# A macaron block on one core: the guard of the front chunks on ScalarE and GpSimd, four score banks in the last two units, and low parts by a minus-identity matmul

## The reference

```python
x = x + 0.5 * ffn(layernorm(x))     # base 512x512 + bias, and 8 LoRA experts of rank 16, top 2 by a softmax router
x = x + attn(layernorm(x))          # 32 query heads, 8 key/value heads of size 16, softmax over 1024 keys
x = x + 0.5 * ffn(layernorm(x))     # the same weights again

def bitnet_linear(x, weight, scale_param):          # q, k, v and o of the attention
    s = jnp.maximum(jnp.mean(jnp.abs(weight), axis=1), 1e-08)
    y = jnp.einsum('bsi,oi->bso', x, jnp.sign(weight / s[:, None])) * (s * scale_param)[None, None, :]
    return jnp.nan_to_num(y, nan=0.0, posinf=1000000.0, neginf=-1000000.0)
```

## Time and profile before

| what | value |
|---|---|
| median of 3 runs | 1210.61 us (1208.24 to 1212.01) |
| the profiled execution's own time | 1210.39 us |
| its span, first to last instruction | 1208.6 us |
| alone stage, to the first exponential of body 0 | 0 to 238.4 us |
| bodies 0 and 1 | about 119 us each |
| bodies 2 to 6 | about 112 us each |
| units 30 and 31 | 1088.9 to 1140.9 us |
| tail | 1140.9 to 1208.6 us |

### The profile page before, as it was taken

One profiled execution on the slowest core, in us unless ns is written; L12 is line 12 of the kernel. 1 busy time (PEld: TensorE's weight loads), 2 busy tenths in 40 slices (PEclk: granted clock), 3 DMA queues, 4 the chain that ended last, 5 costly groups with the idle time before them and its releaser, 6 DMA issues.

```text
span 1208.6 us, 19276 instructions
## 1 busy us (share of the span) xinstructions
PE 1081.1 (89%) x5944; PEld 491.6 (41%) x5944; DVE 876.0 (72%) x1259; ACT 708.4 (59%) x1313; POOL 306.2 (25%) x527
## 2 busy tenths in 40 slices
PE   1877676699999999999999999999999999999857
PEld 1666564334433342334333433443343334333336
DVE  3676869677787778787778777868886787782164
ACT  2343432365776667676667666756765676668511
POOL 4134345610241033141032104210510241032010
PEclk9997989699999999999999999999999999999968
DMA  7012133121121111300300021103101200200300
...
DMA packets 87331, 59.03 MB, mean 49 GB/s; under 512 B 44144, under 2 KB 73328, under 8 KB 87280
## 3 DMA queue, kind: packets, MB, share of 16 engines
...
...
## 4 chain that ended last, share of the span: by engine, by line
PE 73%; DVE 16%; ACT 5%; issue 3%; POOL 1%; DMA 1%; SPq 0%; DVEq 0%; ACTq 0%; POOLq 0%
PE ps_out L1226 19%; PE ps_score L1214 18%; PE ps_max L1193 15%; PE ps_fill L1151 6%; DVE neg_max L1015 3%; PE ps_fill L1178 2%; DVE neg_max L1073 2%; ACT probs L786 2%; PE ps_fill L1124 2%; PE ps_out L1151 2%; PE ps_fill L1155 1%; DVE xt_l L968 1%; DVE zd L927 1%; PE ps_fill L1136 1%; PE ps_max L1207 1%
## 5 line engine op out<-in xcount | busy, mean ns | idle before, releaser
L786 ACT ACTIVATE probs<-ps_score 128x512 f32<-128x512 f32 x1024 | 555.8, 595 | 275.1 <-PE ps_score L1214 273.5
L1015 DVE TENSOR_REDUCE neg_max<-ps_max 128x1 f32<-128x1024 f32 x480 | 571.4, 1218 | 175.7 <-PE ps_max L1193 174.6
L1214 PE MATMUL ps_score<-qst,kst 99*128 99x512 bf16 x1024 | 319.8, 386 | 11.0 <-ACT probs L786 7.8
L1193 PE MATMUL ps_max<-kst,qst 96*128 96x512 bf16 x1024 | 290.0, 384 | 20.7 <-DVE neg_max L1073 12.4
L1226 PE MATMUL ps_out<-probs,v_ring 128*32 128x512 f32 x2048 | 274.5, 608 | 0.0
L1214 PEld LDWEIGHTS ps_score<-qst,kst 99*128 99x128 bf16 x1024 | 88.1, 97 | 287.6 <-ACT probs L786 243.5
L1193 PEld LDWEIGHTS ps_max<-kst,qst 96*128 96x128 bf16 x1024 | 89.2, 98 | 137.5 <-DVE neg_max L1073 21.8
L307 POOL TENSOR_TENSOR wait_pad<-wait_pad 1x1 bf16<-1x1 bf16 x75 | 16.3, 217 | 395.9 <-DVE neg_max L1015 335.0
L1226 PEld LDWEIGHTS ps_out<-probs,v_ring 128*32 128x32 f32 x2048 | 40.4, 108 | 90.7 <-issue 90.3
L1124 PE MATMUL ps_fill<-ident,xn 128*128 128x128 f32 x192 | 32.1, 292 | 37.1 <-ACT xn L735 25.7
L735 ACT ACTIVATE xn<-xc,ln_shift,rstd 128x512 f32<-128x512 f32 x48 | 38.1, 810 | 41.0 <-POOL ln_shift L574 40.5
...
## 6 DMA issues: line engine op xcount, KB each, us to landing
...
```

What stands on the lines that cost most here:

```text
L786: act.activation(probs[:, kt % 2, j, :], ps_score[j % 2][:, :], ACT.Exp, scale=1.0 / HD ** 0.5).then_inc(probs_ready, 1)
L1015: dve.tensor_reduce(neg_max[:, uu % 2, t:t + 1], ps_max[max_slot(uu, pos)][:, :, :], AXY, ALU.max, negate=True).then_inc(max_read, 1)
L1193: last = pe.matmul(ps_max[slot][:, half, :], qst[0:SR, r, j, q * P:(q + 1) * P], kst[0:SR, r, half * 512:half * 512 + 512], start=True, st ...
L1214: pe.matmul(ps_score[j % 2][:, :], kst[0:SR + PARTS, uu, kt * P:(kt + 1) * P], qst[0:SR + PARTS, uu, j, :], start=True, stop=True).then_in ...
```

## The change

- **Guard of front chunks.** ACT evicts to `zd` instead of `z`, and at C0, C1, C2 writes `z` = minus `zd` (one more ACT instruction of 512 columns). POOL makes `zneg` = clamp of `zd` to `[-BIG, 0]`, `zpos` (the same place as `z`) = clamp of minus `zd` to `[-BIG, 0]`, their difference, and the mask as `zd` times 0. Both clamps are now of the form min, then max. DVE keeps only the predicated copy. This holds for all front chunks: `FRONT_ON_DVE` is empty. S1 and S3 on POOL are three instructions of 512, 512 and 256 columns.
- **Low parts outside the bodies** (alone stage and tail): PE adds minus identity times `xt_h` to the bank, and ACT copies the result to `xt_l`. DVE has no part in it.
- **Units 30 and 31**: scores 2 and 3 of a slot go to the free half of `ps_max`; a score waits for the exponential four before it.
- **Opening**: ACT casts the FFN weights after T1b of chunk 0.0, DVE makes their low parts before the statistics of chunk 0.1. POOL writes `neg_ident`.

```diff
-FRONT_ON_DVE = ("clamp", "sum")
+FRONT_ON_DVE = ()
+        def four_score_banks(i, uu):
+            return isinstance(i, int) and UB * i + uu >= NU - 2
+        def score_bank(i, uu, j):
+            if four_score_banks(i, uu) and j >= 2:
+                return ps_max[1 - turn_slot(uu, True)][:, j - 2, :]
+            return ps_score[j % 2][:, :]
...
+            gp.tensor_scalar(neg_ident[:, :], ident[:, :], -1.0, None, ALU.mult).then_inc(const_ready, 1)
...
+                if ch.front:
+                    gp.wait_ge(negated[s], ch.n * 3 + piece + 1)
+                    gp.tensor_scalar(zneg[s][:, cols], zd[s][:, cols], 0.0, -BIG, ALU.min, ALU.max).then_inc(clamped[s], 1)
+                    gp.tensor_scalar(zpos[s][:, cols], z[s][:, cols], 0.0, -BIG, ALU.min, ALU.max).then_inc(clamped[s], 1)
+                    return
...
+                if ch.front:
+                    gp.tensor_tensor(zpos[s][:, cols], zneg[s][:, cols], zpos[s][:, cols], ALU.subtract).then_inc(clamp_sum[s], 1)
+                    return
...
+                    not_finite(ch, k)
...
+                    for a0 in range(0, KQ, 512):
+                        piece = slice(a0, min(a0 + 512, KQ))
+                        rest = kq[:, piece] if k == 1 else parts[s][:, 2, piece]
+                        last = gp.tensor_tensor(rest, kq[:, piece], parts[s][:, k - 1, piece], ALU.subtract)
...
+                if ch.alone and pos[2:] in ("al", "bl"):
+                    stage, t = pos[:3], "ab".index(pos[2])
+                    act.wait_ge(low_ready[s], ch.low0 + ch.tn(stage) + 1)
+                    act.activation(xt_l[s][:, :, t * P:(t + 1) * P],
+                                   ps_fill[ch.bank(stage)[0]][:, :].rearrange("p (c n) -> p c n", c=DC),
+                                   ACT.Copy).then_inc(filler_read[ch.bank(stage)[0]], 1)
...
+                if pos in ("C0", "C1", "C2") and ch.front:
+                    k = int(pos[1])
+                    cols = slice(512 * k, 512 * k + 512)
+                    bnk, reads = ch.bank(("VK", "Q0", "Q1")[k])
+                    act.wait_ge(filler_read[bnk], reads + 1)
+                    act.activation(z[s][:, cols], zd[s][:, cols], ACT.Copy, scale=-1.0).then_inc(negated[s], 1)
...
-                if step[0] == "G" and ch.front:
-                    dve.wait_ge(clamp_sum[s], ch.sum0 + (k + 1))
-                    dve.tensor_scalar(mask, z[s][:, cols].bitcast(I32), INF_BITS, INF_BITS, ALU.bitwise_and,
-                                      ALU.bitwise_xor).then_inc(guard_step[s], 1)
...
-                        dve.copy_predicated(zd[s][:, cols], mask, z[s][:, cols]).then_inc(guard_step[s], 1)
+                        dve.copy_predicated(zd[s][:, cols], mask, zpos[s][:, cols]).then_inc(guard_step[s], 1)
...
+                if ch.alone and pos[2:] in ("al", "bl"):
+                    stage, t = pos[:3], "ab".index(pos[2])
+                    pe.wait_ge(xt_h_ready[s], ch.t0 + ch.tn(stage) + 1)
+                    pe.matmul(ps_fill[ch.bank(stage)[0]][:, :].rearrange("p (c n) -> p c n", c=DC), neg_ident[:, :],
+                              xt_h[s][:, :, t * P:(t + 1) * P], start=False, stop=True,
+                              skip_group_check=True).then_inc(low_ready[s], 1)
+                    return
...
+                if four_score_banks(i, uu) and kt == 0 and j >= 2:
+                    pe.wait_ge(max_read, max_use(i, 1, 16) + 1 if uu == 2 else turn_use(i, 2, True) + 1)
+                elif four_score_banks(i, uu) and kt > 0:
+                    pe.wait_ge(probs_ready, i * (32 * UB) + (32 * uu + 4 * kt + j - 3))
```

More of the change, by code:

```diff
@@ L37 @@
 BIG = 1e6
-INF_BITS = 0x7F800000
 KQ = CH + DC * CH
@@ L154, in macaron @@
         identb = sb("identb", [P, P], BF16)
+        neg_ident = sb("neg_ident", [P, P], F32R)
         ones = sb("ones", [P, P], F32)
@@ L217, in macaron @@
         z = [t[:, 0:ZW] for t in zm]
+        zpos = z
         zneg = [t[:, ZW:2 * ZW] for t in zm]
@@ L271, in macaron @@
         bias_added = [sem(f"bias_added{s}") for s in range(2)]
+        low_ready = [sem(f"low_ready{s}") for s in range(2)]
         xt_h_ready = [sem(f"xt_h_ready{s}") for s in range(2)]
@@ L280, in macaron @@
         guard_step = [sem(f"guard_step{s}") for s in range(2)]
+        negated = [sem(f"negated{s}") for s in range(2)]
+        mask_ready = [sem(f"mask_ready{s}") for s in range(2)]
         part_cast = [sem(f"part_cast{s}") for s in range(2)]
@@ L620, in not_finite @@
                 gp_wait(gp, clamp_sum[s], ch.sum0 + (piece + 1))
-                gp.tensor_scalar(zneg[s][:, cols], z[s][:, cols], 0.0, 0.0, ALU.mult, ALU.add).then_inc(guard_step[s], 1)
+                value = zd[s] if ch.front else z[s]
+                gp.tensor_scalar(zneg[s][:, cols], value[:, cols], 0.0, 0.0, ALU.mult, ALU.add).then_inc(mask_ready[s], 1)
             def fill(item):
@@ L635, in fill @@
                     clamped_sum(ch, k)
-                    if not ch.front:
-                        not_finite(ch, k)
-                if pos in ("G0", "G1", "G2") and ch.on_dve("clamp") and not ch.on_dve("sum"):
-                    clamped_sum(ch, int(pos[1]))
+                    not_finite(ch, k)
                 if pos in ("S1", "S3") and not ch.on_dve("split"):
@@ L711, in _, with ffn_weights @@
         def _(act):
-            act.wait_ge(ffn_in, 5 * 16)
-            act.activation(wr_hl[:, :, 0:E], wr_raw[:, :, :], ACT.Copy).then_inc(ffn_hi, 1)
-            for dst, src in ((a_h, raw_a), (wb_h, raw_wb), (b_h, raw_b)):
-                act.activation(dst[:], src, ACT.Copy).then_inc(ffn_hi, 1)
+            def ffn_weights():
+                act.wait_ge(ffn_in, 5 * 16)
+                act.activation(wr_hl[:, :, 0:E], wr_raw[:, :, :], ACT.Copy).then_inc(ffn_hi, 1)
+                for dst, src in ((a_h, raw_a), (wb_h, raw_wb), (b_h, raw_b)):
+                    act.activation(dst[:], src, ACT.Copy).then_inc(ffn_hi, 1)
             def attn_weights():
@@ L758, in fill @@
                         act.wait_ge(parts_stored[s], n * (16 * 2 * PARTS))
-                    act.activation(z[s][:, 0:CH], ps[:, 0:CH], ACT.Copy, scale=col_scale[:, 0:1])
-                    act.activation(z[s][:, CH:2 * CH], ps[:, CH:2 * CH], ACT.Copy,
+                    act.activation(zd[s][:, 0:CH], ps[:, 0:CH], ACT.Copy, scale=col_scale[:, 0:1])
+                    act.activation(zd[s][:, CH:2 * CH], ps[:, CH:2 * CH], ACT.Copy,
                                    scale=col_scale[:, 1:2]).then_inc(filler_read[bnk], 1)
@@ L766, in fill @@
                         a0 = 512 + (m0 + m) * CH
-                        last = act.activation(z[s][:, a0:a0 + CH], ps[:, m * CH:(m + 1) * CH], ACT.Copy,
+                        last = act.activation(zd[s][:, a0:a0 + CH], ps[:, m * CH:(m + 1) * CH], ACT.Copy,
                                               scale=col_scale[:, 2 + m0 + m:3 + m0 + m])
                     last.then_inc(filler_read[bnk], 1)
+                if pos in ("C0", "C1", "C2") and ch.front:
[4 more added lines that the diff above has]
+                    act.activation(z[s][:, cols], zd[s][:, cols], ACT.Copy, scale=-1.0).then_inc(negated[s], 1)
                 if pos == "VT":
@@ L775, in fill @@
                 if pos == "S0":
-                    act.wait_ge(guard_step[s], ch.guard0 + 6)
+                    act.wait_ge(guard_step[s], ch.sum0 + 3)
                     act.activation(parts[s][:, 0, :], zd[s][:, CH:CH + KQ], ACT.Copy).then_inc(part_cast[s], 1)
@@ L785, in exp_tile @@
                     act.wait_ge(probs_used, i * (8 * UB) + (8 * uu + kt - 1))
-                act.activation(probs[:, kt % 2, j, :], ps_score[j % 2][:, :], ACT.Exp,
+                act.activation(probs[:, kt % 2, j, :], score_bank(i, uu, j), ACT.Exp,
                                scale=1.0 / HD ** 0.5).then_inc(probs_ready, 1)
@@ L809, in _ @@
                 fill(item)
+                if item[0].n == 0 and item[1] == "T1b" and item[0].slot == 0:
+                    ffn_weights()
                 if item[0].n == 0 and item[1] == "FFa0" and item[0].slot == 0:
@@ L962, in fill @@
                                           ALU.add).then_inc(bias_added[s], 1)
-                if pos in ("T0al", "T0bl", "T1al", "T1bl", "T2al", "T2bl"):
+                if pos in ("T0al", "T0bl", "T1al", "T1bl", "T2al", "T2bl") and not ch.alone:
                     stage = pos[:3]
@@ L1075, in _ @@
                 fill(item)
-                if item[0].n == 0 and item[0].slot == 1 and item[1] == "LN1c":
+                if item[0].n == 0 and item[0].slot == 0 and item[1] == "T1bl":
                     ffn_weights()
@@ L1091, in _ @@
         def _(pe):
-            pe.wait_ge(const_ready, 12)
+            pe.wait_ge(const_ready, 13)
             def sum_o():
@@ L1123, in fill @@
                     for c in range(DC):
-                        last = pe.transpose(ps[:, c * P:(c + 1) * P], xn[s][:, t, c * P:(c + 1) * P], ident[:, :])
```

(5 more changed lines are left out.)

22 lines of the change are left out of this document (10 added, 12 removed).

## The result

| | before | changed |
|---|---|---|
| median | 1211.31 us (1208.24 to 1212.99, 4 runs) | 1228.01 us (1227.08 to 1231.27, 4 runs) |
| ratio | | 1.0147, 95% interval 1.0129 to 1.0165 |
| the profiled execution, its span | 1210.39, 1208.6 | 1231.27, 1229.4 |

The kernel became 16.7 us slower, where I had forecast 8: the direction was right, the size was not, and 1228 lies outside my range.

What follows compares the result with a forecast made beforehand. DVE was taken to bound the guard stretches and the row maxima. The terms -4.0 + 1.4 + 13.4 - 2.2 - 0.5 - 4.3 + 4.5 gave +8.3 on 1210.39, forecast 1219 us; range 1205 to 1226.

Steps and rivals of the forecast that it cites:

- C: Guard stretch, VK to the next pair's FFa, twice: POOL's longer queue adds 6.7 us each, +13.4.
- R2: Rival, faster: DVE's relief ends the router's chain and FFa earlier; about 1205 us, chance 0.18.
- R3: Rival, worse: POOL pays contention every time, PE's clock drops; C +9.5 each, 1224.5 us; chance 0.13 together with R4.
- R1: Rival, the queue's floor: C is only what POOL must do, +2.9 each; 1211 us, chance 0.19.
- R4: Rival: the four banks give nothing because ACT is the bound there; 1223 us, chance 0.13 together with R3.
- B: Low part by PE and ACT, pairs 0 and 1: a longer path, 2 x 0.7 = +1.4 us.
- A: Opening: ACT normalises before casting weights, DVE's low weights start earlier; -4.0 us after 0.75 for low parts.
- D: Third pair, under the row maxima: DVE's chain loses low parts and masks, -2.2 us.
- E: Bodies 0 and 1: DVE loses three masks each, ACT gains three instructions; -0.5 us.
- F: Units 30 and 31: four banks let two scores run early; a bare slot saves 0.35, in all -4.3 us.
- G: Tail: the low part is on the path six times and PE's order makes it wait; +4.5 us.

Runs made afterwards that it cites:

- e10: The changed kernel with the predicated copies of pairs 0 and 1 cut to 64 of 512 columns: 1223.32 us, ratio 1.0110.
- e6: The changed kernel with the bias additions of pairs 0 and 1 meant for DVE (pair 2's, in the second stretch, stayed on POOL): 1222.12 us, ratio 1.0110.
- e5: The kernel before with only the low parts outside the bodies moved to PE and ACT: 1209.16 us, ratio 0.9982.
- e2: The kernel before with the new guard alone, without the new low parts, opening or four banks: 1232.05 us, ratio 1.0168.
- e4: The kernel before with the new opening alone: 1205.11 us, ratio 0.9950.
- e7: The changed kernel without POOL's mask instruction in pairs 0 and 1: 1221.62 us, ratio 1.0101.
- e13: The kernel of e8 with pair 0's low parts also on DVE and the old guard in all front chunks: 1199.75 us, ratio 0.9920.
- e8: The kernel of e1 with the tail's low parts back on DVE: 1198.66 us, ratio 0.9896.
- e1: The changed kernel with the guard of pairs 0 and 1 back on DVE: 1205.98 us, ratio 0.9959.

## Why the prediction was right in sign and wrong in size

**C, the guard stretch (forecast +6.7 each, measured +10.9, bound +9).** This is the step that failed, and nearly the whole miss: 2 x 4.2 = 8.4. The queue itself I had right: the norm of chunk 1.1 ends 33.8 us after VK (96.81 + 0.19 - 63.16), of which 2.5 is contention at five POOL instructions, so 31.3 without it against my 31.8. Two terms were mis-sized. Contention on POOL: I "took half" of 0 to 2.8, and it was 2.5, paid every time, as e10 shows. Contention on DVE: I wrote no term for it. From the norm to FFa I had 11.0; it took 14.4, and 3.7 of that is what P2, `w_tmp` and `w_rep` lose beside POOL's bias and split (e6). The path there was not the one I named either: I had S0 and a low part on ACT behind P2, 1.9 us, and it goes by `w_tmp`, `w_rep` and WR, as it did before the change. Without contention these take about 2, so the wrong path cost nothing in that sum, by luck; but it hid the two DVE instructions behind P2, which could be delayed. My step "what DVE gains only turns into waiting" stopped there: the instructions that remain on DVE are fewer but stand on the path, and beside them POOL has no pause from 78.4 to 106.2. The row that announced it was in my own list, the cast of four columns that took 2.19; I used it for R2, as a price that would vanish, and not for C, as a price that would be paid more often.

From the Trainium skill's rule ("SBUF — State Buffer", "Who interferes with whom") I had drawn that a copy delays either itself or POOL, never both. The trace agrees with the exclusion but not with that reading: at 81.77 the copy lost 1.1 to the first addition, and the second addition then 0.5 to the copy. Of the rivals R3 came nearest, with contention paid every time; but it put it on POOL and on PE's clock, not on DVE, and its price was still too low (9.5). R1, R2 and R4 fell.

**B, low part by PE and ACT (+1.4).** One low part on PE's path costs 0.46 more than before (from the start of `xt_h` at 61.33 to VK at 63.16 is 1.83, against 1.37 in the earlier trace rows), where I had 0.35. For pair 1 the 0.7 didn't come: from FFa to VK of chunk 1.0 it took 21.9, against 22.8 before. And I left out that a low part off DVE can give time: where DVE has the guard, e5's stretches are 1.4 shorter than before. In the changed kernel's stretch it is neither: 48.3 without (e2), 48.2 with.

**A, opening (-4.0).** The -4.0 holds 1.15 for low parts, so it is -5.15 for e4, which showed -5.5. In the changed kernel VK of 0.0 came 2.2 earlier, forecast 3.3 with the first half of B; one slow burst (below) took 1.7, more than the shortfall, and e7, without it and with the same opening, is at 61.8, -3.6. Right.

**D (-2.2) and E (-0.5).** -2.5 and, over all bodies to the `o_sb` of unit 29, -0.6 (852.3 to 851.7). Right in the sum, but e2, e5 and e13 show that the gain of D belongs to neither part alone, and I had added it up part by part.

**F (-4.3).** -2.6, within the bounds. The bare slot is what I said, 2.57 against 2.89 in the earlier trace rows; exponentials of unit 31 in the changed kernel:

```profile
1135.24 1.09 ACT L823 ACTIVATE probs<-ps_max 128x512 f32<-128x512 f32 x2 [0.71 <-PE ps_max L1264]
...
1137.81 1.08 ACT L823 ACTIVATE probs<-ps_max 128x512 f32<-128x512 f32 x2 [0.49 <-PE ps_max L1264]
...
1140.37 1.09 ACT L823 ACTIVATE probs<-ps_max 128x512 f32<-128x512 f32 x2 [0.49 <-PE ps_max L1264]
```

But a slot filled with FFa or FFb is mostly PE's: by the starts of the exponentials six of the 16 slots took the same before and after, the longest of 4.08 among them, and two fell only from 3.6 to 3.4. I had given such slots 0.3 instead of nothing or 0.2.

**G, tail (+4.5).** +5.2, gone in e8. Right, though e1 and e5 had 74.1 and 75.3, +6.4 and +7.6, for which no run has a cause.

**Sum.** -2.2 + 2 x 10.9 - 2.5 - 0.6 - 2.6 + 5.2 = +19.1, and the two parts from FFa behind a stretch to the next VK 1.8 (one of them slow, 2.4): 20.9, against 20.8 between the spans.
